# Early-fusion block on one core: no warm-up products, the start regrouped, keys and corrections moved, loops written out

## What is computed

```
h   = concat(cls token, patches(x) @ tok_W + tok_b + tok_pos)      # 50 rows per image
h   = concat(h, txt)                                               # 178 rows of 192
xn  = layernorm(layernorm(h), ln_w)
Q_h = xn * W_qk[h]                     for 12 heads h              # queries are the keys
out_h = softmax(causal(Q_h @ Q_h.T / sqrt(192))) @ (xn - mean(wte)) / (row number)
h   = h + concat(out_h) @ W_o.T
y   = layernorm(h)
w   = 4 of 16 experts (best 4 of 8 groups, then best 4 experts), scaled by 2.5
h   = h + sum_e w_e * expert_e(y) + shared_expert(y)
```

## Time and profile before

| | |
|---|---|
| median of 3 runs | 488.14 us (487.24 to 488.76) |
| the profiled execution | 487.14 us |
| its span, first to last instruction | 485.3 us |
| PE busy | 457.4 us (94%) |
| DVE busy | 294.2 us (61%) |
| ACT busy | 175.0 us (36%) |
| POOL busy | 102.4 us (21%) |
| mean granted TensorE clock | 0.988 of full speed |

### The profile page before, as it was taken

How to read it: one execution, slowest core, us unless ns; L and a number is a source line. 1 busy time by engine, 2 the same in 40 slices (tenths; PEclk the granted TensorE clock), 3 DMA queues, 4 the chain that set the end, 5 groups by cost and what they waited for, 6 DMA issues and landing times. The chain is left out here.

```text
span 485.3 us, 7575 instructions
## 1 busy us (share of the span) xinstructions
PE 457.4 (94%) x2672; PEld 390.6 (80%) x2672; DVE 294.2 (61%) x814; ACT 175.0 (36%) x573; POOL 102.4 (21%) x111
## 2 busy tenths in 40 slices
PE   5688999999999999899998998999999999999997
PEld 2465667967679766597766998998999899989996
DVE  6775777258673586744586718576746574654443
ACT  1364457144571334732435024452222222121221
POOL 6031111111112111000012104850261026100000
PEclk9898999999999999999999999999999999999999
DMA  8979999999999999966007022223222222223230
GB/s 205 245 251 211 205 210 211 212 211 212 213 213 213 213 213 214 189 122 231 0 1 268 2 63 46 64 57 75 75 58 63 73 76 61 60 74 74 71 67 26
DMA packets 23679, 64.90 MB, mean 134 GB/s; under 512 B 2876, under 2 KB 13332, under 8 KB 23266
## 3 DMA queue, kind: packets, MB, share of 16 engines
q0 software_dynamic: 7904, 40.86, 40.2%
q1 hardware_dynamic: 14882, 22.68, 17.7%
q10 hardware_dynamic: 864, 1.00, 0.8%
HBM read 61.88 MB, written 1.27 MB: 130 GB/s over the span
## 5 line engine op out<-in xcount | busy, mean ns | idle before, releaser
L515 ACT ACTIVATE pm<-bank,nmax 128x128 f32<-128x128 f32 x96 | 34.0, 366 | 113.0 <-DVE nmax L1009 113.0
L791 PE MATMUL bank<-woT,area_o 128*128 128x192 f32 (+1 forms) x432 | 71.4, 327 | 0.0
L1098 DVE TENSOR_TENSOR area_b<-area_b,area_w 128x356 f32<-128x356 f32 x64 | 33.9, 529 | 61.1 <-ACT area_b L585 60.9
L791 PEld LDWEIGHTS bank<-woT,area_o 128*128 128x128 f32 (+1 forms) x432 | 70.0, 182 | 0.4
L422 POOL DMA_DIRECT2D area_w<-in_L_attn_wte_dram x26 | 31.4, 1207 | 133.1 <-DMA area_w<-in_L_attn_wte_dram 133.1
L870 PE MATMUL bank<-area_w_r,area_o_r 128*128 128x356 f32 x112 | 43.9, 392 | 0.0
L738 PE MATMUL bank<-pT,xn 128*128 128x356 f32 x96 | 38.9, 486 | 4.5 <-ACT pT L528 3.0
L585 ACT ACTIVATE area_b<-bank,area_k 128x356 f32<-128x356 f32 x32 | 17.9, 559 | 60.9 <-PE bank L874 60.9
L906 PE MATMUL bank<-area_k,area_b 128*128 128x192 f32 (+1 forms) x192 | 37.0, 328 | 1.4 <-DVE area_b L1110 1.4
L871 PE MATMUL bank<-area_w_r,area_o_r 128*128 128x356 f32 x112 | 36.4, 325 | 0.0
L541 ACT ACTIVATE area_b<-xb,w 64x192 f32<-64x192 f32 x96 | 34.2, 459 | 0.0
(11 more groups left out here) (218 smaller groups left out, 1001.9 us busy)
## 6 DMA issues: line engine op xcount, KB each, us to landing
area_w<-in_L_attn_wte_dram POOLq DMA_DIRECT2D x28, 1344.0 KB, 12.7
area_w<-gate_rows SPq DMA_DIRECT2D x64, 178.0 KB, 3.0
area_k<-in_experts_dram SPq DMA_DIRECT2D x8, 353.0 KB, 5.6
area_a<-in_experts_dram SPq DMA_DIRECT2D x6, 353.0 KB, 5.5
woT<-in_L_attn_W_o_dram SPq DMA_DIRECT2D x1, 1728.0 KB, 16.0
area_o<-in_x_dram SPq DMA_DIRECT2D x4, 384.0 KB, 9.8
area_w<-area_w POOLq DMA_DIRECT2D x1, 1344.0 KB, 9.8
area_b<-in_experts_dram SPq DMA_DIRECT2D x3, 353.0 KB, 7.2
```

The source lines that it names most:

```text
L515: last = act.activation(pm[:, sl, j, :], bank[0][:, j * P:(j + 1) * P], ACT.Exp, bias=nmax[:, sl, j:j + 1], accum_out=psums[:, sl, j:j + 1])
L791: last = pe.matmul(o, oT[:, c, at:at + n], woT[:, c, :], start=(c == 0), stop=(c == NCH - 1))
L1098: dve.tensor_tensor(sil[:, n % 2, :], sil[:, n % 2, :], wbc[:, m % RING, :], ALU.mult).then_inc(weighted, 1)
```

## The change

The 16 products and the wait for the constants ahead of the first `embed` go. On ACT's queue the transfer of `w2` goes behind those of `postab` and `tokb`, and on DVE the work on `w2` and `lnw` goes between `norm_begin` and `norm_end`; `embeds_out(1)` comes after `norm_end`. `embed(2)` and `embed(3)` (now in banks 4 and 7) go from behind `scores(0, 0)` into units 0 and 1 of pair 0, as do `embeds_out(2)`, `embeds_out(3)` and `norm_begin` of pair 1. The queries of the second item (`queries(1, 1)`, `queries_b(1, 1)`) go from ahead of pair 0 into its units 0 to 2, one group in each; pair 1's `norm_end` goes from unit 1 to unit 2. In each of the first three pairs `turn_in(0, ..)` comes after `turn_probs(3)`, and `keep(0, ..)` with the first group of queries goes from the end of unit 3 into unit 4, ahead of `tails_out(4)`. `correct(1)` goes from the first expert step to unit 4 of the last pair, `correct(2)` and `correct(3)` from step 0 of the pair before theirs to step 14 of the one before that, POOL's `rstd` with them. The loops on PE, ACT and DVE are written out.

```diff
@@ -32,9 +32,6 @@
         self.n += 1
-
-    def restart(self, base):
-        self.base, self.n = base, 0
 
@@ -61,7 +58,6 @@
     SCALE = float(E) ** -0.5
-    WARM = 16
     WROWS = V // P
@@ -175,7 +171,7 @@
         wts = sb("wts", [P, NT, NW])
-        emb_bank = [bank[n] for n in (6, 5, 3, 2)]
+        emb_bank = [bank[n] for n in (6, 5, 4, 7)]
         in_a = area_a.shape[1] // WX
@@ -473,6 +469,7 @@
             x_low_b(0)
+            rstd(3, PAIRS + 2)
             w_low(2)
@@ -484,8 +481,8 @@
                     if i + 1 < PAIRS:
-                        if k == 0:
-                            rstd(3, PAIRS + i + 2)
+                        if k == 14 and i + 2 < PAIRS:
+                            rstd(3, PAIRS + i + 3)
                         if k == 3:
@@ -497,9 +494,9 @@
             act.dma_start(wtok[:], tok_W).then_inc(s_tokw, 16)
-            act.dma_start(w2[:], W_qk.rearrange("p (c h) -> p c h", c=2)).then_inc(s_small, 16)
             act.dma_start(postab[:], tok_pos).then_inc(s_pos, 16)
             act.dma_start(tokb[:], tok_b.rearrange("(a e) -> a e", a=1).broadcast_to([P, E])).then_inc(s_pos, 16)
+            act.dma_start(w2[:], W_qk.rearrange("p (c h) -> p c h", c=2)).then_inc(s_small, 16)
             act.dma_start(lnw[:], ln_w.rearrange("(a e) -> a e", a=1).broadcast_to([P, E])).then_inc(s_small, 16)
@@ -551,8 +548,6 @@
             queries_b(0, 0, [2])
-            act.wait_ge(xnT_ready, 4)
-            queries_b(1, 1, range(UPB))
 
@@ -590,9 +585,12 @@
                         mix_out(u - 1, U + u - 1)
+                    prob_out(u, U + u)
+                    if i == 0 and u < UPB:
+                        act.wait_ge(xnT_ready, 4)
+                        queries_b(1, 1, [u])
                     if u == 3 and not last:
                         turn_out(0, 2 * i + 2)
-                    prob_out(u, U + u)
                     if u == 3 and last:
@@ -615,7 +613,7 @@
 
-            with act.Fori(0, PAIRS - 1) as i:
+            for i in range(PAIRS - 1):
                 pair(i, False)
@@ -645,12 +643,6 @@
 
-            pe.wait_ge(s_const, 1)
-
-            for _ in range(WARM):
-                pe.matmul(bank[0][:, :], identb[:], cmask[:].rearrange("p (a t) -> p a t", a=1).broadcast_to([P, GRP, P]),
-                          start=True, stop=True)
-
             def embed(i):
@@ -661,10 +653,13 @@
             embed(1)
+            pe.wait_ge(s_const, 1)
 
                 pe.wait_ge(z_ready, 2 * i + b + 1)
+                if i == 1:
+                    pe.wait_ge(s_hin, PAIRS)
                 if not isinstance(bt, int) or bt:
@@ -726,6 +721,8 @@
                         pe.wait_ge(proj_read, 3 * i)
+                if U == 0:
+                    pe.wait_ge(s_hin, 3)
                 if u % UPB == 0:
@@ -799,8 +796,6 @@
             scores(0, 0)
-            embed(2)
-            embed(3)
 
@@ -829,8 +824,11 @@
                         mix(u - 1, U + u - 1, i)
-                    if u == 3 and not last:
-                        turn_in(0, 2 * i + 2, i + 1)
+                    if i == 0 and u == 0:
+                        embed(2)
+                    if i == 0 and u == 1:
+                        pe.wait_ge(xnT_ready, 4)
+                        embed(3)
                     if u == 1 and last:
@@ -838,6 +836,8 @@
                     turn_probs(u, U + u)
+                    if u == 3 and not last:
+                        turn_in(0, 2 * i + 2, i + 1)
                 mix(4, U + 4, i)
@@ -857,8 +857,7 @@
             pe.wait_ge(s_wo, 16)
-            pe.wait_ge(s_hin, PAIRS)
-            with pe.Fori(0, PAIRS - 1) as i:
+            for i in range(PAIRS - 1):
                 pair(i, False)
@@ -948,11 +947,6 @@
             own.mark(dve.tensor_scalar(nnreg[:], nreg[:], -1.0, None, ALU.mult))
-            dve.wait_ge(s_small, 32)
-            dve.scalar_tensor_tensor(out=w2[:], in0=w2[:], scalar=SCALE, in1=w2[:], op0=ALU.mult,
-                                     op1=ALU.mult).then_inc(s_w2, 1)
-            dve.wait_ge(s_w2, 1)
-            link(dve.tensor_scalar(lnw[:], lnw[:], (1.0 + EPS) ** -0.5, None, ALU.mult))
             dve.wait_ge(s_pos, 32)
@@ -1063,7 +1057,7 @@
 
-                dve.wait_ge(proj_read, 3 * (PAIRS if i == PAIRS - 1 else PAIRS - 1))
+                dve.wait_ge(proj_read, 3 * (PAIRS if i > 1 else PAIRS - 1))
                 tiles = tiles_of(i)
@@ -1122,18 +1116,19 @@
             norm_begin(hin[:, 0:2])
+            dve.wait_ge(s_small, 32)
+            dve.scalar_tensor_tensor(out=w2[:], in0=w2[:], scalar=SCALE, in1=w2[:], op0=ALU.mult,
+                                     op1=ALU.mult).then_inc(s_w2, 1)
+            dve.wait_ge(s_w2, 1)
+            link(dve.tensor_scalar(lnw[:], lnw[:], (1.0 + EPS) ** -0.5, None, ALU.mult))
+            norm_end(0, hin[:, 0:2])
             embeds_out(1)
-            norm_end(0, hin[:, 0:2])
-            queries(0, 0)
+            queries(0, 0, [0])
             keep(0, 0)
             keep(1, 0)
-            dve.wait_ge(s_text[1], 64)
-            dve.wait_ge(s_hin, 2)
-            norm_begin(hin[:, 2:4])
+            queries(0, 0, [1])
             maxima(0, 0)
-            embeds_out(2)
-            embeds_out(3)
-            queries(1, 1)
+            queries(0, 0, [2])
 
@@ -1202,7 +1197,18 @@
                         mix_out(u - 1, U + u - 1)
+                    if i == 0 and u < 2:
+                        embeds_out(2 + u)
+                    if u == 4 and not last:
+                        keep(0, i + 1)
+                        queries(0, 2 * i + 2, [0])
                     tails_out(u, U + u)
+                    if i == 0 and u < UPB:
+                        queries(1, 1, [u])
+                    if i == 0 and u == 0:
+                        dve.wait_ge(s_text[1], 64)
+                        dve.wait_ge(s_hin, 2)
+                        norm_begin(hin[:, 2:4])
                     if sums:
@@ -1229,13 +1235,12 @@
                             experts_in(0)
+                        if u == 4:
+                            correct(1)
                     if not last:
 
-                        if u == 1:
-                            norm_end(i + 1, hin[:, 2 * i + 2:2 * i + 4] if isinstance(i, int) else hin[:, bass.ds(2 * i + 2, 2)])
-                        if u == 3:
-                            keep(0, i + 1)
-                            queries(0, 2 * i + 2, [0])
+                        if u == (2 if i == 0 else 1):
+                            norm_end(i + 1, hin[:, 2 * i + 2:2 * i + 4])
                         if u == 4:
@@ -1249,7 +1254,7 @@
 
-                        norm_begin(hin[:, bass.ds(2 * i + 4, 2)])
+                        norm_begin(hin[:, 2 * i + 4:2 * i + 6])
                 else:
@@ -1261,14 +1266,8 @@
 
-            start = own.at
-            per = UPP + (4 + 4) + 4
-            with dve.Fori(0, PAIRS - 2) as i:
-                own.restart(per * i + start)
-                pair(i, False, True)
-                assert own.n == per
-            own.restart(start + per * (PAIRS - 2))
-            pair(PAIRS - 2, False, False, True)
+            for i in range(PAIRS - 1):
+                pair(i, False, i + 2 < PAIRS, i + 2 == PAIRS)
             pair(PAIRS - 1, True, False)
@@ -1283,8 +1282,6 @@
                     if i + 1 < PAIRS:
-                        if k == 0:
-                            correct(i + 1)
                         if k == 1:
@@ -1296,6 +1293,8 @@
                             choose_experts(i + 1)
+                        if k == 14 and i + 2 < PAIRS:
+                            correct(i + 2)
             finish(PAIRS - 1)
```

## The result

The changed kernel takes 482.6 us (median; 480.0 to 483.7 in four runs), against 488.5 for the kernel before (four runs, three of them the ones in the table of its time): a ratio of 0.987, 95% interval 0.983 to 0.992. A second session with five runs gave 480.3 and 0.9865 (0.984 to 0.989). The forecast was 481.5 and a range of 479.2 to 485.6.

What follows compares the result with a forecast made beforehand. PE, busy 94% of the span, was taken as the bound, with time won only where it waits, repeats work or runs at half clock. -2.9-5.0+0.1+2.25+0.3-1.4 = -6.65 takes 488.14 to 481.5 us, range 479.2 to 485.6.

Steps and rivals of the forecast that it cites:

- Start, -2.9: Start up to scores(0): without the 16 products it comes 2.9 us earlier, at 18.8; ends 2.0 and 3.0.
- To `mix(0)`: From scores(0) to mix(0): 5.0 us less, about 2.9 of waits, 1.8 of half clock, 0.3 of the rest.
- Unit 4, +1.0+1.0+0.25: Unit 4 of pairs 0 to 2: keep and one query group delay the copies for mix(4), 2.25 us more.
- Last pair, +0.3: Unit 4 of the last pair: the correction before divide(5) costs 0.3 us; ends 0 and 2.45.
- Experts, -1.4: First expert steps: moving the correction away removes PE's waits of 0.84 and 0.59, 1.4 us less; ends 0.8 and 1.8.
- POOL, 0: POOL's fold of the wte sum moves from 207.0 to at most 211.3, still in time for DVE: cost 0.
- Loops, 0: Loops written out on PE, ACT and DVE: taken as 0, by the skill's rule up to 0.19 us gained.
- rival 4: Written-out code is fetched behind full DMA queues, stopping PE and DVE: 9 to 12 us, 491; chance 0.05.
- Rivals 1 to 3: DVE bounds pair 0: 484.0, chance 0.14; start not earlier: 483.9, 0.08; wte sum late to last pair: 483.5, 0.06.

Runs made afterwards that it cites:

- the two fastest versions: Changed kernel, keep and queries before mix_out(3), late woT wait, 7 and 5 fill products: 475.4 us; or with 7, 8, 2, 3 and mean split: 476.5 us.
- all together: The changed kernel with keep and first queries before mix_out(3), mean's products in three places, 7 and 5 fill products, woT wait at first project: 477.6 us, 0.9786.

## Why the prediction was right

The prediction's steps, by its own terms:

- **Start, -2.9** (ends -2.0 and -3.0): measured -2.24 and -3.04, at the ends it gave. The first `embeds_out` came at 10.04 for the 10.4 forecast, bound by DVE's L949, which stands beside POOL's memset as before. `embed(1)` runs at half clock in both profiles, so that is not what parts the two ends, as the prediction had it. It is the landing of the second patches: 11.93 in the first profile, and in the second 11.07, so that `embed(1)` ends at 15.2 instead of 16.1 and the transposes run at full clock:

```profile
11.07 4.15 PE L650 MATMUL bank<-wtok,area_o 128*128 128x192 f32 x12 [1.30 <-DMA area_o<-in_x_dram]
15.39 0.30 PE L665 MATMUL bank<-ident,z 128*128 128x128 f32 x1 [0.18 <-DVE z L984]
```
- **To `mix(0)`**: forecast at 35, measured 35.41. No row waits on `hin`, `scores(2)` runs at full clock. From `scores(0)` to `scores(1)` the prediction took ACT's exponentials as the bound, 6.7 us; measured 6.60 and 6.15, with 0.6 to 1.2 us of wait for ACT in it. Ahead of `scores(5)` PE waits 0.32 for the 0.1. From `scores(0)` to `scores(5)` the gain is 4.83 us in the first profile and 5.28 in the second, for 4.9 in the sum. Undoing this part costs 5.7 us by medians and 5.8 by the profile up to `mix(4)`, so the 5.0 had about the right size.
- **Unit 4, +1.0+1.0+0.25**: measured +1.08, +0.97 and +0.33 (after less before, from `scores(5)` to `mix(4)` in pair 0, from the pair's `scores(1)` to `mix(4)` in the two others). The mechanism, `keep` and one group ahead of the copies, is shown by the experiment that moves them.
- **Last pair, +0.3**: +0.25 at `mix(5)`. A wait of 0.36 us for DVE's probabilities of unit 5 in pair 2 was not in the sum; from `mix(4)` to `mix(5)` of that pair it costs 0.44.
- **Experts, -1.4** (ends 0.8 and 1.8): this term was too small. From the start of the experts to the end it is 196.2 us for 198.1, -1.9; putting the corrections back costs 1.87 there. I had named the longer reading as an end (1.8) and then taken the waits as printed.
- **POOL, 0**: the fold at 210.18, forecast 210 to 211.5, and DVE's use of it at 224.16 without a wait.
- **Loops, 0**: shown. The instruction packets rose by the seven that q8 and q14 have more (36 for 29; I had estimated six), and no wait came of them, so rival 4 has nothing to stand on. The Trainium skill's rule on branches ("Runtime: NRT & Kernel Launch", "Instruction fetch mechanics") made at most 0.19 us of gain, too little to be seen here.

The sum of -6.65 stands between the two profiles, -4.3 and -7.3, and between the differences of medians, -5.9 and -7.3. That it came out well has a share of luck: of the fall behind the mean (1.7 us where it comes) no term spoke. Without it the span is 478.0, 0.65 us more gained than the sum: 0.55 in the experts and 0.1 at the start, while 0.4 more won in pair 0 and 0.4 more lost between `mix(4)` of pair 2 and the experts cancel. Rivals 1 to 3 didn't happen: DVE's room in pair 0 sufficed, the start came forward, and the fold was early enough.

On the removed warm-up the Trainium skill ("TensorE: Matmul & The Clock Gate", "What's actually happening") was weighed with half clock for `embed(0)`, and the trace agrees: 4.21 us for 2.07. That the products would pay elsewhere is what the fill experiments show: ahead of the first embedding they cost, and in the gaps ahead of `scores(0)` they win 1.9 us where they hold the clock (spans 473.5 for 475.4 with the late wait for `woT` alone). The prediction had said that a faster clock in `scores(0)` would win nothing, since the wait for `woT` is the floor; that held only as long as this wait stood ahead of pair 0.

## What to carry to other kernels

Put products that only keep the clock up into gaps that PE has anyway, and not ahead of the first real work, where they cost 2.9 us here. With two gaps filled, `scores(0)` kept the full clock in four or five of ten executions by their spans; with all gaps up to it filled, in at least four of five. When work moves into a unit, place it behind the copies for which PE is due next; one exchange of two calls was worth 2.9 us by the traces, as much as the whole start. Price a wait of PE by the distance of starts to an undisturbed repetition, not by the wait as printed.

## What the runs showed that I had not expected

- PE can be 100% busy and still fall to the lower level, 1.2 GHz: behind 30 products of one column (2.3 us, 230 to 232), granted 0.50, 1.7 us lost. It comes in some executions of a kernel and not in others, and a moved wait at 24 us that shifted the work by a fraction of a microsecond went with none of five for four of five. What decides stays open.
- The granted clock reads 1.00 in all windows of the changed kernel's first profile up to 232 us, yet 12 products of 192 columns take 4.21 us there at 5.58 and at 11.93, and 2.18 at 29.34, and `scores(0)` at 19.48 takes 2.05 us for two rows that otherwise take 1.02. The profiles of the two fastest versions read 1.00 throughout and have `embed(0)` at 4.21 and 4.09 us. So ahead of its first change the record of these profiles can't be trusted, nor can the mean clock that is taken from it; durations can.
- A gap of 1.74 us was followed by a fall at two of the 15 places that have it (1.2 and 1.6 us lost), and at the others not.
- Three DVE operations took 1.82 us for 1.06 beside the same POOL operation, which itself took 1.21 for 1.47: one of the two pays, POOL in nine profiles and DVE in one. The Trainium skill ("SBUF — State Buffer", "Who interferes with whom") has the two engines share a port by an exclusive lock, for operations like these with two inputs in SBUF, and says that the order of issue decides who is blocked. The lengths agree with one waiting for the other. The order isn't shown: POOL's operation starts 0.39 us behind the first of the three in the profile in which DVE pays and in that of all together, in which POOL does.
